# Moving the ten "low half" subtractions of the normalised rows from VectorE to GpSimd, and to another place in the written schedule

## Chip, cores and metric

One core of one Trainium2 chip runs the whole layer in one launch. The metric is the device time of the kernel in microseconds; lower is better.

## What is computed

x has 1250 rows (nodes) of 512. There are 20000 edges, `src` to `dst`, sorted by `dst`. Cut to what matters:

```python
xn  = layernorm(x)
agg = segment_sum(xn[src], dst)              # sum over the edges
h   = (1 + eps) * xn + agg
h   = relu(batch_norm(h @ W1 + b1)); h = relu(batch_norm(h @ W2 + b2))
q, k, v = elu(xn @ Wq + bq) + 1, elu(xn @ Wk + bk) + 1, xn @ Wv + bv
z   = 1 / (q . sum(k))                       # per head, 8 heads of 64
mix = (q @ (k^T v) * z) @ Wp + bp             # linear attention
x   = x + (xn + h) + mix
x   = x + moe(layernorm(x))                   # 64 experts, top 2 by hash
```

## The kernel before

**The front part.** Nodes lie in 10 row tiles (`NT`) of 128 (the last has 98). `XN` holds the normalised rows, `XT` their transpose. The aggregation is not a gather: for groups of edge tiles the kernel builds one-hot matrices and multiplies them into a matrix of edge counts `AT16` (1250 by 1250, 16 bit), and then multiplies the rows of x with it. The steps around the change:

- `oh` g (L965, on VectorE): one-hot of the destination key of edge group g, 16-bit `tensor_scalar`, one instruction for each edge tile of the group. For every third group the one-hot of the source, L969, is on VectorE too; for the others it is on ScalarE (L1362, L1365). `atm` g (L596, TensorE): their product. `ata` g (L984, VectorE): adds it from PSUM into `AT16`.
- K's products (`kmm` L562), `kadd` (L943) and `phi` (L949) on VectorE make phi(k). `phi` i also is a step of GpSimd: the running sum over the tiles, `KSUM` (L1536). `gmm` (L570) is the product of x's rows with phi(k).
- `ks` (L580, L585): sums of k on TensorE, after the last GpSimd addition. `ksc` (L953, L954): their copy from PSUM by VectorE; it frees the bank that the first product of Q needs.
- `qmm` (L607): Q's products, 12 units of four; `qphi` (L992) on VectorE ends each.
- `z` c (L618) and `zr` c (L1010): the denominators of attention and their reciprocal on VectorE, for each of three column chunks `CH` of 418, 416 and 416 nodes. `zb`, `zm` (L1023), `qzh`, `qzl` (L1028): z is spread and multiplied into Q.
- `xh` i (L1348, ScalarE): the row tile rounded to the reduced type float32r, `XNH`. `xl` i (L1002, VectorE): `XNL = XN - XNH`, the low half, 128 by 512. It is written where `XN` lies, so it has to wait for the `gmm` of its tile.
- `conv` (L1402, ScalarE) rounds the counts of a tile. `agg` c, i (L636, L637): eight products of tile i for chunk c, with `XNH` and with `XNL`. `ht` (L1035) takes the sums from PSUM.

**What sets the order.** `front_schedule` gives every step a due time, sorts the list, and every engine walks through the list and executes those of its steps that stand in it, in order. A due time orders and starts nothing: what starts a step is its semaphores and the engine being free. Numbers in it: K's products start at 12.0 with 6.0 for a tile, so `done` is 77.7; Q's units take 2.7 each; `agg` is due from `first` = 112.7, every 1.5. `xl` i is due at `base + turn * i - 1.7`, 111.0 and on, between the reciprocals. The last `phi` step is due before `done`.

The second part (from about 216 us) is the two dense layers with batch norm, the routing, and the experts with their weights streamed by SyncE's queue.

Of the kernel before, what the change touches and what calls it, by code (L numbers as in the profile page):

```python
# [11 lines left out]
ALU = mybir.AluOpType  # L12
# [4 lines left out]
NT = 10  # L17
# [21 lines left out]
def rows(i):  # L39
    return min(128, N - 128 * i)  # L40
# [30 lines left out]
def front_schedule():  # L71


    due = []

    def at(t, *step):
        due.append((t, len(due), step))

    begin, pair, unit, turn = 12.0, 6.0, 2.7, 1.5
    spent = 0  # L80
    at(11.2, "prep", 0)
    at(50.0, "prep", 1)
    work = [m * (33 + w) + 2 * (16 + w) for _, m, w in GRP]
    for g, w in enumerate(work):
        t = 13.6 + 96 * spent / sum(work)
        spent += w
        at(t - 2.3, "oh", g)
        at(t, "atm", g)
        at(t + 0.8, "ata", g)
    for i in range(NT):  # L90
        at(8.3 + 1.7 * i, "st", i)
    for q, (a, b) in enumerate(BATCH):
        at(8.3 + 1.7 * (b - 1) + 0.5, "sq" if q < ROOTS else "nwt", q)
        at(8.3 + 1.7 * (b - 1) + (0.9 if q < ROOTS else 5.0), "rr", q)
    for i in range(NT):
        k = begin + pair * i
        xt = k - (3.0 if i else 1.5)
        at(xt - 1.2, "xn", i)
        at(xt, "xt", i)
        at(xt + 1, "xtc", i)  # L100
        for q in range(4):
            at(k + pair * q / 8, "kmm", i, q)
            at(k + pair * (1.45 + q / 8), "gmm", i, q)
        at(k + pair / 2 + 0.3, "kadd", i)
        at(k + pair / 2 + 1.2, "kexp", i)
        at(k + pair / 2 + 2.4, "phi", i)
        at(k + pair / 2 + 3.2, "xh", i)
    done = begin + pair * (NT + 0.95)
    at(done + 0.1, "ks")
    at(done + 0.2, "gts")  # L110
    at(done + 0.9, "ksc")
    for u in range(12):
        t, r, c = done + 2.2 + unit * u, u % 4, u // 4
        for q in range(4):
            at(t + unit * q / 4, "qmm", r, c, q)
        at(t + unit + 0.2, "qact", r, c)
        at(t + unit + 1.9, "qphi", r, c)
    first = max(done + 2.2 + 12 * unit, 111.5) + 0.4
    at(first - 4.0, "flag")
    at(first - 2.5, "flagd")  # L120
    for c in range(3):
        base = first + 10 * turn * c
        for i in range(NT):
            if c == 0:
                at(base + turn * i - 1.7, "xl", i)
            at(base + turn * i - 2.0, "conv", c, i)
            at(base + turn * i, "agg", c, i)
        zb = base + (3.5 if c else 2.5)
        at((first - 7, first - 3.5, first + 9)[c], "z", c)
        at((first - 6, first - 2.5, first + 10)[c], "zr", c)  # L130
        at(zb, "zb", c)
        for r in range(4):
            t = zb + 1 + 1.6 * r
            at(t, "zm", r, c)
            at(t + 0.7, "qzh", r, c)
            at(t + 1.6, "qzl", r, c)
            t = base + 10 * turn + 0.5 + 0.8 * r
            at(t, "ht", r, c)
            at(t + 0.5, "hth", r, c)
            at(t + 1.04, "htl", r, c)  # L140
    last = first + 30 * turn
    at(last - 11, "kvt")
    at(last - 7.4, "kvd")
    for r in range(4):
        at(last - 6 + 0.9 * r, "m", r)
        at(last - 5 + 0.9 * r, "mh", r)
        at(last - 4 + 0.9 * r, "ml", r)
    at(last + 0.3, "wide")
    at(last + 4.2, "widev")
    for i in range(NT):  # L150
        at(last + 0.4 + 2.6 * i, "p", i)
        at(last + 4.3 + 2.6 * i, "pa", i)
    for t in range(8):
        at(last + 4.4 + 2.6 * t, "w1h", t)
        at(last + 5.4 + 2.6 * t, "w1l", t)
    return [step for _, _, step in sorted(due)]
# [101 lines left out]
def gnn_mix_moe(nc, x_in, edg_in, chk_in, wcol_in, low_in, w1g, w2g, wqkvp, hp_in, vec_in, brow_in, cst_in, we_in, out):  # L258
# [4 lines left out]
    with ExitStack() as ctx:  # L263
# [7 lines left out]
        V, A, G = nc.vector, nc.scalar, nc.gpsimd  # L271
# [9 lines left out]
        def big(first, size):  # L281
            return BIG1[:, first:first + size] if first < SPLIT else BIG2[:, first - SPLIT:first - SPLIT + size]

        def rounded(first, size):
            q = max(k for k in range(len(ROUND)) if cuts[k] <= first)
            return ROUND[q][:, first - cuts[q]:first - cuts[q] + size]

        def by(ap, k):
            return ap.rearrange("p (k n) -> p k n", k=k)
# [49 lines left out]
        XN, XNL, XNH = by(big(XN0, 5120), NT), by(rounded(XN0, 5120), NT), by(rounded(XN0 + 5120, 5120), NT)  # L339
        XNHf, XNLf = XNH.bitcast(F32), XNL.bitcast(F32)  # L340
# [122 lines left out]
        plan = bank_plan(order)  # L463
# [5 lines left out]
        full = [sem(f"full{b}") for b in range(8)]  # L469
# [407 lines left out]
        def vector(dve):  # L877
            done = [0]
# [12 lines left out]
            for step in order:  # L891
                kind = step[0]
# [27 lines left out]
                elif kind == "st":  # L920
                    i, n = step[1], rows(step[1])
# [12 lines left out]
                elif kind == "kadd":  # L934
                    i = step[1]
# [9 lines left out]
                elif kind == "phi":  # L945
                    i, n = step[1], rows(step[1])
# [9 lines left out]
                elif kind == "oh":  # L956
# [4 lines left out]
                    if g >= OHG:  # L961
                        b, use = at_of(("at", g - OHG))
# [23 lines left out]
                elif kind == "qphi":  # L986
                    r, c = step[1:]
                    o, w = CH[c]
                    b, use = at_of(("q", r, c))
# [1 line left out]
                    dve.wait_ge(moved[b], use)  # L991
                    V.scalar_tensor_tensor(QT[:, r, o:o + w], TMP[:, 2 * (r % 2) + 1, 0:w], 1.0, QT[:, r, o:o + w], ALU.min,  # L992
                                           ALU.max).then_inc(s_q, 1)
                elif kind == "xl":
                    i, n = step[1], rows(step[1])
                    dve.wait_ge(s_xh, i + 1)
                    if i < NT - 1:
                        dve.wait_ge(s_g, i + 1)
                    else:
                        b, use = plan["gts"][3]  # L1000
                        dve.wait_ge(full[b], use)
                    V.tensor_tensor(XNL[0:n, i, :], XN[0:n, i, :], XNHf[0:n, i, :], ALU.subtract).then_inc(s_xl, 1)  # L1002
                elif kind == "zr":
                    c = step[1]
                    b, use = at_of(("z", c))
# [5 lines left out]
                elif kind == "flagd":  # L1011
                    b, use = at_of(("flag",))
# [30 lines left out]
                elif kind == "kvd":  # L1043
                    b, use = at_of(("kvt",))
# [86 lines left out]
            for t in range(4):  # L1131
# [7 lines left out]
                if t == 1:  # L1139
                    b, use = at_of("hpm")  # L1140
# [45 lines left out]
            for step in route_order():  # L1186
                kind = step[0]
                if kind == "am":
                    a, e = ARGMAX[step[1]]
                    m = slice(4 * a, 4 * e)  # L1190
                    b, use = at_of(("lg", e - 1))
# [10 lines left out]
            b, use = at_of("near")  # L1202
# [8 lines left out]
            b, use = at_of("slots0")  # L1211
# [5 lines left out]
            for q, (i, e) in enumerate(((0, 8), (8, NT))):  # L1217
                b, use = at_of(f"below{q}")
# [84 lines left out]
            for i in range(NT + 1):  # L1303
                if i < NT:
                    n = rows(i)
# [212 lines left out]
        def gpsimd(pool):  # L1518
# [7 lines left out]
            for step in order:  # L1526
                kind = step[0]
                if kind == "phi":
                    i, n = step[1], rows(step[1])
                    u = PHI[i % 4][0:n, :]  # L1530
                    pool.wait_ge(s_phi, i + 1)
                    if i == 0:
                        G.tensor_copy(KSUM[:, :], u).then_inc(s_ksum, 1)
                    else:
                        pool.wait_ge(s_ksum, i)
                        G.tensor_tensor(KSUM[0:n, :], KSUM[0:n, :], u, ALU.add).then_inc(s_ksum, 1)  # L1536
                elif kind == "nwt":
                    q, w = slice(*BATCH[step[1]]), BATCH[step[1]][1] - BATCH[step[1]][0]
                    v, t, half, y = NWV[:, 0, 0:w], NWV[:, 1, 0:w], NWV[:, 2, 0:w], RR[:, q]
                    done = NEWTON * (step[1] - ROOTS)  # L1540

                    def newton(ins):
                        nonlocal done
                        done += 1
                        ins.then_inc(s_nwt, 1)
                        pool.wait_ge(s_nwt, done)

                    pool.wait_ge(s_st, BATCH[step[1]][1])
                    newton(G.tensor_scalar(v, MV[:, q, 1], 0.5, 0.5e-5, ALU.mult, ALU.add))
                    newton(G.tensor_scalar(y.bitcast(I32), v.bitcast(I32), -0.5, float(0x5f3759df - 2 ** 22), ALU.mult, ALU.add))  # L1550
                    for _ in range(3):
                        newton(G.tensor_tensor(t, y, y, ALU.mult))
                        newton(G.tensor_tensor(t, t, v, ALU.mult))
                        newton(G.tensor_tensor(t, half, t, ALU.subtract))
                        newton(G.tensor_tensor(y, y, t, ALU.mult))
                elif kind == "wide":
                    pool.wait_ge(s_key, NKEY["flag"])
                    far = pool.value_load(FLAGI[0:1, 0:1], min_val=0, max_val=2000)
                    with pool.If(far >= WIN):
                        wide_pool(pool)  # L1560

            b, use = at_of(("m", 3))
# [4 lines left out]
            b, use = at_of(("h1", 7, 2))  # L1567
# [24 lines left out]
            b, use = at_of("slots0")  # L1592
# [6 lines left out]
            b, use = at_of("slots")  # L1599
            pool.wait_ge(moved[b], use)  # L1600
            pool.wait_ge(sd_yz, 16 * 20)
            for r in range(32 - LATE):
                scatter_pair(r)
                n = r + LEAD
# [399 lines left out]
```

## Time and profile before

| what | value |
|---|---|
| device time, median of 3 runs | 557.75 us (556.35 to 559.13) |
| profiled execution | 558.88 us, span 557.1 us |
| granted clock of TensorE, mean | 0.994 of full speed |
| busy: TensorE, VectorE, ScalarE, GpSimd | 524.2, 348.0, 253.1, 92.7 us |
| moved by DMA | 105.69 MB, mean 190 GB/s |

Busy times are sums over the whole span. An engine that is busy 94% of it sets the time; the others matter through what it waits for. Since the stages have different limits, the table tells little of one stage: that is read from the rows below.

### The profile page before, as it was taken

The numbers are of one execution on the slowest core, as the hardware profiler recorded it, in microseconds if no ns is written. First come the engines' busy times: TensorE is split into PE (matmuls) and PEld (weight loads), VectorE is DVE, ScalarE is ACT, GpSimd is POOL, SyncE is SP. The second block draws the span as 40 slices with busy tenths as digits, with TensorE's granted clock in tenths as the row PEclk, the third lists the DMA queues.
The fourth block names the chain that finished last, engine by engine and source line by source line (L and its number), as shares of the span: only waits on it lengthen the run. The fifth ranks groups of instructions, "written<-read, shape, count | busy, mean of one in ns | idle before, by whom it ended". The sixth has DMA issues, their size and how long they took to land.

```text
span 557.1 us, 8514 instructions
## 1 busy us (share of the span) xinstructions
PE 524.2 (94%) x2810; PEld 362.6 (65%) x2810; DVE 348.0 (62%) x981; ACT 253.1 (45%) x554; POOL 92.7 (17%) x119
## 2 busy tenths in 40 slices
PE   0799999999998999999999999997999999999997
PEld 0344444455488888899999999985555554545545
DVE  4888787767876545638888234388344445344767
ACT  2787766676544533125665222347333334333300
POOL 4141101100000000000000000003144444445310
PEclk9999999999999999999999999999799999999999
DMA  8500000000020006465007322987999999999978
GB/s 301 209 2 1 1 1 1 1 1 0 2 77 0 1 0 214 166 237 207 2 0 281 136 75 77 349 348 278 338 406 416 414 415 412 413 416 415 400 267 310
DMA packets 32409, 105.69 MB, mean 190 GB/s; under 512 B 4640, under 2 KB 10017, under 8 KB 25324
## 3 DMA queue, kind: packets, MB, share of 16 engines
q1 hardware_dynamic: 22364, 86.09, 39.8%
q0 software_dynamic: 4880, 9.78, 4.7%
q10 hardware_dynamic: 5120, 9.25, 4.7%
q8 instruction: 24, 0.39, 0.3%
q14 instruction: 21, 0.17, 0.1%
HBM read 93.48 MB, written 17.84 MB: 200 GB/s over the span
## 4 chain that ended last, share of the span: by engine, by line
PE 77%; DMA 8%; DVE 7%; issue 5%; POOL 1%; DVEq 1%; ACT 1%; SPq 0%; POOLq 0%; ACTq 0%
PE PS L533 8%; PE PS L532 8%; PE PS L534 8%; PE PS L834 7%; PE PS L848 6%; PE PS L607 6%; DMA BIG<-xx_rows,TIDX 6%; PE PS L570 5%; PE PS L562 5%; PE PS L636 4%; PE PS L637 4%; PE PS L753 3%; PE PS L596 3%; PE PS L824 2%; DMA KSUM<-xx_rows,TIDX 2%
## 5 line engine op out<-in xcount | busy, mean ns | idle before, releaser
L532 PE MATMUL PS<-ROUND 128*128 128x416 f32 (+3 forms) x232 | 83.8, 361 | 0.0
L533 PE MATMUL PS<-ROUND 128*128 128x416 f32 (+3 forms) x232 | 83.5, 360 | 0.0
L534 PE MATMUL PS<-ROUND 128*128 128x416 f32 (+3 forms) x232 | 83.4, 359 | 0.0
L848 PE MATMUL PS<-BIG 128*64 128x512 f32 x208 | 52.8, 592 | 0.2 <-DVE BIG L1271 0.2
L1085 DVE BATCH_NORM_STATS2 BST<-BIG 128x6 f32<-128x416 f32 (+1 forms) x36 | 20.7, 590 | 44.0 <-ACT BIG L1448 35.5
L636 PE MATMUL PS<-ROUND 128*128 128x416 f32 (+3 forms) x120 | 43.5, 363 | 2.3 <-DVE ROUND L1002 1.8
L984 DVE TENSOR_TENSOR BIG<-PS,BIG 128x280 f32 (+17 forms) x69 | 30.7, 445 | 23.4 <-PE PS L596 19.4
L532 PEld LDWEIGHTS PS<-ROUND 128*128 128x128 f32 (+1 forms) x232 | 43.6, 188 | 2.6
L534 PEld LDWEIGHTS PS<-ROUND 128*128 128x128 f32 (+1 forms) x232 | 43.6, 188 | 2.5
L533 PEld LDWEIGHTS PS<-ROUND 128*128 128x128 f32 (+1 forms) x232 | 43.5, 188 | 2.4
L965 DVE TENSOR_SCALAR BIG<-BIG 128x180 f16<-128x180 f16 (+20 forms) x157 | 43.1, 321 | 0.0
L637 PE MATMUL PS<-ROUND 128*128 128x416 f32 (+3 forms) x120 | 42.2, 351 | 0.0
L562 PE MATMUL PS<-BIG 128*128 128x512 f32 (+1 forms) x80 | 41.3, 628 | 0.7 <-ACT BIG L1344 0.7
L570 PE MATMUL PS<-BIG 128*128 128x512 f32 (+1 forms) x80 | 39.9, 596 | 0.0
L596 PEld LDWEIGHTS PS<-BIG 128*128 128x128 f16 x157 | 14.1, 98 | 37.7 <-issue 23.6
L607 PE MATMUL PS<-BIG 128*128 128x416 f32 (+1 forms) x96 | 37.4, 515 | 0.2 <-DVE KSUM L953 0.2
L1289 DVE TENSOR_TENSOR BIG<-PS,BIG 128x512 f32<-128x512 f32 x21 | 14.5, 689 | 33.7 <-PE PS L848 33.7
L1480 ACT ACTIVATE BIG<-BIG 128x512 f32<-128x512 f32 x24 | 15.1, 629 | 43.7 <-DMA BIG<-xx_rows,TIDX 43.6
L1362 ACT ACTIVATE BIG<-BIG 128x128 f16<-128x128 f16 x103 | 34.6, 389 | 0.4 <-PE PS L596 0.4
L596 PE MATMUL PS<-BIG 128*128 128x180 f16 (+20 forms) x157 | 28.3, 274 | 4.8 <-DVE BIG L984 3.4
L834 PE MATMUL PS<-BIG,KSB 128*64 128x256 f32 x208 | 29.0, 405 | 0.7 <-issue 0.7
L1579 POOL DMA_INDIRECT y_rows<-BIG,SCIDX x21 | 22.0, 1050 | 43.4 <-DVE BIG L1289 43.4
(271 smaller groups left out, 967.5 us busy)
## 6 DMA issues: line engine op xcount, KB each, us to landing
BIG<-in_we SPq DMA_DIRECT2D x46, 1024.0 KB
BIG<-in_we SPq DMA_DIRECT2D x12, 512.0 KB
y_rows<-KVB SPq DMA_DIRECT2D x19, 256.0 KB
BIG<-y_rows SPq DMA_DIRECT2D x9, 512.0 KB, 9.2
EXTRA<-in_we SPq DMA_DIRECT2D x4, 1024.0 KB
XA<-in_we SPq DMA_DIRECT2D x4, 1024.0 KB
BIG<-in_wqkvp ACTq DMA_DIRECT2D x3, 1024.0 KB, 15.0
XA<-in_we SPq DMA_DIRECT2D x6, 512.0 KB
```

Source lines behind the costliest of these rows:

```text
L532: mm(o, ah, bh, start=first, stop=False)
L533: mm(o, ah, bl, start=False, stop=False)
L534: return mm(o, al, bh, start=False, stop=last)
L562: ins = mm(PS[0:n, b, :], XT[:, k, cs], WK[:, k, :], start=(k == 0), stop=(k == 3))
L570: ins = mm(PS[:, 4 + k, :], XN[0:n, i, 128 * k:128 * k + 128], PHI[i % 4][0:n, :], start=(i == 0), stop=(i == NT - 1))
L596: ins = mm(PS[:, b, 0:NT * w], SRCOH[:, g % OHG, q, :], KEYOH[:, g % OHG, NT * w * q:NT * w * (q + 1)], start=(q == 0), stop=(q == m - 1))
L607: ins = mm(PS[:, b, 0:w], WQ[:, k, f], XT[:, k, o:o + w], start=(k == 0), stop=(k == 3))
L636: mm(PS[:, b, 0:w], XNH[0:n, i, f], ATR[j % 3][0:n, 0:w], start=(i == 0), stop=False)
L637: ins = mm(PS[:, b, 0:w], XNL[0:n, i, f], ATR[j % 3][0:n, 0:w], start=False, stop=(i == NT - 1))
L834: ins = mm(PS[64 * j:64 * j + 64, b, 0:256], XTT[s][:, 128 * k + 64 * j:128 * k + 64 * j + 64], weights(2 * r + j, 256 * k, 256), start=(k ...
L848: ins = mm(PS[64 * j:64 * j + 64, b, :], HT[:, s, 128 * f2 + 64 * j:128 * f2 + 64 * j + 64], weights(2 * r + j, 1024 + 512 * f2, 512), sta ...
L965: V.tensor_scalar(KEYOH[:, g % OHG, NT * w * q:NT * w * (q + 1)], IOTA16[:, 0:NT * w], KEYF[:, t0 + q:t0 + q + 1], None, ALU.is_equal).the ...
```

## The change

In the schedule the ten `xl` get other due times: `done + 2.4 + 2.7 * i`, that is 80.1 and on, one for each of the first ten units of Q's products. And the step moves, with its waits unchanged, from VectorE's program to GpSimd's.

```diff
             if c == 0:
-                at(base + turn * i - 1.7, "xl", i)
+                at(done + 2.4 + 2.7 * i, "xl", i)
...
-                elif kind == "xl":
-                    i, n = step[1], rows(step[1])
-                    dve.wait_ge(s_xh, i + 1)
-                    if i < NT - 1:
-                        dve.wait_ge(s_g, i + 1)
-                    else:
-                        b, use = plan["gts"][3]
-                        dve.wait_ge(full[b], use)
-                    V.tensor_tensor(XNL[0:n, i, :], XN[0:n, i, :], XNHf[0:n, i, :], ALU.subtract).then_inc(s_xl, 1)
...
+                elif kind == "xl":
+                    i, n = step[1], rows(step[1])
+                    pool.wait_ge(s_xh, i + 1)
+                    if i < NT - 1:
+                        pool.wait_ge(s_g, i + 1)
+                    else:
+                        b, use = plan["gts"][3]
+                        pool.wait_ge(full[b], use)
+                    G.tensor_tensor(XNL[0:n, i, :], XN[0:n, i, :], XNHf[0:n, i, :], ALU.subtract).then_inc(s_xl, 1)
```

## Rows read from the trace of the kernel before

**Rows 1.** The page: busy time by engine, and the chain that ended last.
```profile
PE 524.2 (94%) x2810; PEld 362.6 (65%) x2810; DVE 348.0 (62%) x981; ACT 253.1 (45%) x554; POOL 92.7 (17%) x119
...
PE 77%; DMA 8%; DVE 7%; issue 5%; POOL 1%; DVEq 1%; ACT 1%; SPq 0%; POOLq 0%; ACTq 0%
```

**Rows 2.** Busy time by stretch: stretch, its us, then each engine, clock, DMA.
```profile
110.00:152.00 42.00, 41.22 (x147) 20.45 (x145) 31.83 (x82) 24.51 (x57) 0.00 (x0) 1.00 0.00 1
152.00:171.00 19.00, 16.85 (x92) 14.49 (x93) 13.84 (x21) 8.46 (x16) 0.00 (x0) 1.00 0.18 56
171.00:216.00 45.00, 44.34 (x239) 39.57 (x238) 26.96 (x49) 21.48 (x43) 1.03 (x3) 1.00 0.04 11
```

**Rows 3.** Whom TensorE waited for, 100 to 260 us: total, times, longest.
```profile
PE PS L636 <- DVE ROUND L1002: 1.8, 1, 1.8
PE PS L596 <- DVE BIG L984: 1.8, 2, 1.1
```

**Rows 4.** The instructions of line 1002: shortest, median, longest in ns; first and last start.
```profile
L1002 DVE TENSOR_TENSOR ROUND<-BIG,ROUND x10: 627/686/686, 151.6 to 168.5; 128x512 fp32r<-128x512 f32 x9, 98x512 fp32r<-98x512 f32 x1
```

**Rows 5.** Timeline of TensorE: start, us, line and operation, [idle before, released by].
```profile
103.64 0.48 PE L596 MATMUL PS<-BIG 128*128 128x360 f16 x2 [1.11 <-DVE BIG L984]
...
109.53 1.64 PE L607 MATMUL PS<-BIG 128*128 128x418 f32 x4 [0.23 <-DVE KSUM L953]
...
148.83 3.06 PE L607 MATMUL PS<-BIG 128*128 128x416 f32 x8
152.37 0.43 PE L636 MATMUL PS<-ROUND 128*128 128x418 f32 x1 [0.48 <-issue]
...
168.76 0.43 PE L636 MATMUL PS<-ROUND 128*128 128x418 f32 x1 [1.78 <-DVE ROUND L1002]
```

**Rows 6.** Timeline of VectorE around the reciprocals.
```profile
148.96 2.76 DVE L1010 RECIPROCAL KVB<-PS 128x416 f32<-128x416 f32 x1 [0.63 <-PE PS L618]
151.64 0.63 DVE L1002 TENSOR_TENSOR ROUND<-BIG,ROUND 128x512 fp32r<-128x512 f32 x1
...
165.31 2.76 DVE L1010 RECIPROCAL XG<-PS 128x416 f32<-128x416 f32 x1 [1.81 <-PE PS L618]
167.99 1.22 DVE L1002 TENSOR_TENSOR ROUND<-BIG,ROUND 128x512 fp32r<-128x512 f32 x2
```

**Rows 7.** Timeline of GpSimd.
```profile
25.29 0.61 POOL L1553 TENSOR_TENSOR BIG<-BIG 128x3 f32<-128x3 f32 x1
...
26.92 0.19 POOL L1553 TENSOR_TENSOR BIG<-BIG 128x3 f32<-128x3 f32 x1
...
84.00 1.27 POOL L1536 TENSOR_TENSOR KSUM<-KSUM,BIG 128x512 f32<-128x512 f32 x1 [6.24 <-DVE BIG L949]
91.86 1.27 POOL L1536 TENSOR_TENSOR KSUM<-KSUM,BIG 128x512 f32<-128x512 f32 x1 [6.59 <-DVE BIG L949]
101.43 1.52 POOL L1536 TENSOR_TENSOR KSUM<-KSUM,BIG 98x512 f32<-98x512 f32 x1 [8.30 <-DVE BIG L949]
```

**Rows 8.** Timeline of VectorE beside GpSimd's instructions and away from them.
```profile
25.17 0.68 DVE L949 SCALAR_TENSOR_TENSOR BIG<-BIG 128x512 f32<-128x512 f32 x1
...
83.84 1.53 DVE L965 TENSOR_SCALAR BIG<-BIG 128x300 f16<-128x300 f16 x2
...
86.00 0.50 DVE L965 TENSOR_SCALAR BIG<-BIG 128x320 f16<-128x320 f16 x2
...
92.25 0.49 DVE L984 TENSOR_TENSOR BIG<-PS,BIG 128x320 f32 x1 [0.47 <-PE PS L596]
```

**Rows 9.** Timeline of VectorE from 101 us to the copy of k's sum.
```profile
101.27 0.53 DVE L965 TENSOR_SCALAR BIG<-BIG 128x360 f16<-128x360 f16 x2
101.72 1.45 DVE L969 TENSOR_SCALAR BIG<-BIG 128x128 f16<-128x128 f16 x2
...
105.28 0.53 DVE L965 TENSOR_SCALAR BIG<-BIG 128x380 f16<-128x380 f16 x2
...
108.69 0.69 DVE L953 COPY KSUM<-PS 128x512 f32<-128x512 f32 x1 [1.79 <-PE PS L585]
```

## The prediction, made before the change was run

> **What bounds the kernel now.** I read the page first. TensorE is busy 94% of the span, and 77% of the chain that ended last lies on it [rows 1]. So an edit on VectorE or GpSimd moves the end only by making TensorE wait more or less. Next, the stages. In the stretch of Q's products (110 to 152 us) TensorE is busy 41.22 of 42.00 us, and VectorE 31.83, with GpSimd quite idle. In the first aggregation chunk (152 to 171) TensorE is busy 16.85 of 19.00 [rows 2]. Third, the list of who waited for whom between 100 and 260 us: TensorE waited 1.8 us for L984 (VectorE's adds of edge counts, `ata`), with 1.11 us of it just before 103.64, and 1.8 us, once, for L1002, which is `xl`, the operation that moves [rows 3, 5]. Last, the timelines around these waits. The reader is to see two things: VectorE is late in two places of the aggregation because of its long reciprocals, and it is also late just before Q's products, when GpSimd works beside it.
>
> **What the change removes.** Ten subtractions of 0.63 to 0.69 us leave VectorE [rows 4], some 6.9 us of its time. What they cost TensorE is read at two places [rows 5, 6].
>
> The first `agg` product starts at 152.37 after 0.48 us of idle time. On VectorE the reciprocal `zr` 1 runs from 148.96 for 2.76 us, to 151.72, and `xl` 0 comes behind it, from 151.64 to 152.27; TensorE starts 0.10 us later. Q's last products run from 148.83 for 3.06 us, to 151.89, and the reciprocal, which frees a bank that `agg` needs, is done before that. So without `xl` 0 behind the reciprocal, the 0.48 us go.
>
> The second place: `agg` 7 ends at about 168.76 - 1.78 = 166.98, `zr` 2 runs from 165.31 for 2.76 us, and `xl` 8 follows at 167.99; `agg` 8 starts at 168.76 after a wait of 1.78 us. `xl` 9 is then 0.6 us behind and not waited for. Without `xl` this wait goes whole: the converted counts for `agg` 8 come from ScalarE, which is 8.46 us busy in these 19 us [rows 2], and no other VectorE result is asked for there. The gain is 0.48 + 1.78 = 2.26 us. The other eight `xl` cost TensorE nothing, so taking them off VectorE gives nothing more. TensorE is nearly without idle time behind it (44.3 of 45 us in the stretch after 171), so I let the 2.26 us reach the end in full.
>
> **What the change adds.** GpSimd executes its steps in the order of the written schedule. The last step before `xl` on its queue is `phi` 9, the sum of k, which ends at 101.43 + 1.52 = 102.95 [rows 7]. What `xl` 0 to 8 wait for (the rounded copy by ScalarE and the G products on rows 0 to 8) is there by then, and `xl` 9's last G product is over by 107. The due times 2.7 us apart order the queue but start nothing. So the ten do not spread over Q's products: they run one behind the other from 102.95. The nearest row for one is L1536, the same shape with two inputs from SBUF and one output to it: 1.27 us each [rows 7]. Ten are 12.7 us, up to 115.65 or a little later, 36 us before the first `agg` asks. As a result nobody waits for them. No DMA is issued by `xl`, and behind it on GpSimd's queue only `wide` follows, which stays idle for 90 us more.
>
> What they cost is VectorE's time beside them. The pair of one-hots L965 that ran beside the GpSimd addition at 84.00 took 1.53 us, against 0.50 for the pair at 86.00 [rows 7, 8]: the second one stood still until GpSimd's addition ended. The nine additions of the trace all repeat this; beside seven of them, this one among them, the pair is 0.87 to 1.09 us longer. The plain add L984 at 92.25 took its ordinary 0.49 us beside the addition at 91.86: it reads one input from PSUM and is not touched. And the other way round, GpSimd's 3-element multiplication at 25.29 took 0.61 us, against 0.19 at 26.92, while L949 (two inputs from SBUF) ran from 25.17 to 25.85.
>
> The Trainium skill, page "SBUF — State Buffer", section "Who interferes with whom", says that VectorE in a two-port mode, or with two SBUF inputs, and a reading GpSimd instruction exclude each other for a whole instruction, whoever is first. By that page the "free" engine is not free beside `oh`, and the trace agrees (1.53 against 0.50 us).
>
> Where does that land? VectorE's queue at 101.72 still holds, in this order [rows 9]: the pair L969 (1.45 us beside `phi` 9), `ata`, a pair L965, `ata`, a pair, `ata`, two pairs (the L965 at 105.28 and an L969 pair behind it), `ata`, and then L953, the copy of k's sum, at 108.69, for which Q's first product waited 0.23 us [rows 5]. So nine instructions that exclude GpSimd's (one left of L969's pair, and four pairs) stand ahead of the instruction that opens Q's products. VectorE had 1.79 us of idle time just before L953; that is its whole slack.
>
> How GpSimd and VectorE take turns when GpSimd has work without a gap, no row shows. Bounds from both sides:
> - Strict turns: each GpSimd end (104.22, 105.49, ... every 1.27 us) lets one of the nine pass. The ninth passes at 102.95 + 9 x 1.27 = 114.38, the last `ata` takes 0.5, and the copy comes at about 115.0 instead of 108.69: 6.3 us.
> - Pairs pass together, as at 101.27, where two L965 went through and the addition that began at 101.43 came out 0.25 us late [rows 7, 9]. Then five GpSimd instructions at most are waited for. The steps are: L969 at 104.2, `ata`, pair after 105.5, `ata` to 106.4, pair after 106.9, `ata` to 107.9, four L965/L969 after 108.4, `ata`, copy at about 110.0. That is 1.3 us, and the five `xl` left over cost about 0.5 more in the next 6 us, where VectorE has idle stretches of 1.1 and 0.6 us. Sum 1.8 us.
>
> The second of a pair starts 0.22 us behind the first, and its race with the next GpSimd instruction is close: at 84.00 GpSimd won it, at 101.43 VectorE did, with the same spacing. I take half of the pairs split: (6.3 + 1.8) / 2 = 4.05 us. TensorE has no slack in Q's products, so all of it reaches TensorE.
>
> **Sum.** -2.26 + 4.05 = +1.8 us. The profiled execution (558.88 us, span 557.1) goes to about 560.7; it is 1.1 above the median of the runs. On the median 557.75 I forecast 559.5 us. The runs before spread over 2.8 us, 0.5%, and that is about what can be told from no change.
>
> **Rivals.**
> *Nothing reaches TensorE.* The exclusion costs VectorE time but its slack takes it. Against it: TensorE already waits 1.11 us for L984 before 103.64 [rows 5], and what held L984 up is the pair L969 beside a single GpSimd addition. Time: 557.75 - 2.26 = 555.5 us. It decides if the copy L953 starts before about 109.
> *VectorE is locked out until GpSimd's row of ten ends.* One addition leaves a gap today; ten without a wait between them may leave none. VectorE then resumes at 115.65 and has the 3.8 us of work from 103.1 to 106.9 ahead of it, so the copy is at 119.5: 10.8 us late. Time: 557.75 - 2.26 + 10.8 = 566.3 us. Against it: the pair that stood waiting at 101.72 was through, both of it, at 103.17, 0.22 us after GpSimd's end [rows 9], so what waits gets in at the first opening.
> *GpSimd's subtraction is slower than its addition.* Its output is the rounded type, which no GpSimd instruction of this trace has. With 1.6 us in place of 1.27 and strict turns, nine turns add 9 x 0.33 = 3.0 to the 6.3: 557.75 - 2.26 + 9.3 = 564.8 us. It decides by the duration of one `xl` on GpSimd.
>
> **How the numbers follow.** The forecast case, turns that are partly strict, has 0.70, and its own range is the two bounds, 557.3 (-2.26 + 1.8) to 561.8 (-2.26 + 6.3). Nothing reaches TensorE: 0.13. Locked out: 0.08. Slower subtraction: 0.09. The range 555.0 to 564.0 takes in the first rival with the scatter of the runs, and leaves out the lock-out and the worst of the slow subtraction. Slower by over 0.5% (above 560.5): a third of the forecast case (0.23) and most of the last two, 0.38. Faster by over 0.5% (below 555.0) would need more than the whole gain: 0.06. Within: 0.56.
>
> **What the profile after would show.** Ten GpSimd instructions in a row from about 103 to 116 to 118, 1.27 to 1.5 us each. L965 and L969 between 103 and 116 drawn out to over 1 us, L984 not. The copy L953 at 110 to 115, and Q's first product just behind it. No wait of TensorE at the first `agg` and at `agg` 8. The forecast is wrong if the ten are spread out, if VectorE stands still for ten microseconds in one piece, or if the two waits in the aggregation stay under another name.

## The result, and the profile after

The changed kernel takes 563.33 us (median of 6 runs, 561.02 to 565.30), the kernel before 557.54 (6 runs). The ratio is 1.0096, with a 95% interval of 1.0063 to 1.0130: slower by 5.4 us (3.5 to 7.3), where 1.8 were forecast. The two medians alone lie 5.8 us apart. The profiled execution took 562.01 us with a span of 560.2, and its mean granted clock is 0.988, against 0.994 before.

GpSimd's timeline around the moved work, columns as in [rows 7]; L1527 is `phi`, L1536 is now `xl`:

```profile
101.09 1.52 POOL L1527 TENSOR_TENSOR KSUM<-KSUM,BIG 98x512 f32<-98x512 f32 x1 [8.30 <-DVE BIG L949]
102.57 12.34 POOL L1536 TENSOR_TENSOR ROUND<-BIG,ROUND 128x512 fp32r<-128x512 f32 x10
```

The ten run in one row behind `phi` 9 and not over Q's products, and the row has no gap: ten in 12.34 us is 1.22 to 1.23 us from start to start. The instructions themselves:

```profile
L1536 POOL TENSOR_TENSOR ROUND<-BIG,ROUND x10: 1256/1268/1277, 102.6 to 113.6; 128x512 fp32r<-128x512 f32 x9, 98x512 fp32r<-98x512 f32 x1
```

One takes 1.27 us, the duration of the additions of [rows 7]. The rounded output costs nothing, and VectorE delayed none of them: the longest is 0.02 us over the shortest. VectorE beside them, which answers to [rows 9]:

```profile
101.37 2.50 DVE L969 TENSOR_SCALAR BIG<-BIG 128x128 f16<-128x128 f16 x2
103.80 0.50 DVE L984 TENSOR_TENSOR BIG<-PS,BIG 128x340 f32 x1
104.22 2.17 DVE L965 TENSOR_SCALAR BIG<-BIG 128x360 f16<-128x360 f16 x2
106.31 0.52 DVE L984 TENSOR_TENSOR BIG<-PS,BIG 128x360 f32 x1
106.76 2.10 DVE L965 TENSOR_SCALAR BIG<-BIG 128x360 f16<-128x360 f16 x2
108.78 0.52 DVE L984 TENSOR_TENSOR BIG<-PS,BIG 128x360 f32 x1
109.22 2.12 DVE L965 TENSOR_SCALAR BIG<-BIG 128x380 f16<-128x380 f16 x2
111.27 2.47 DVE L969 TENSOR_SCALAR BIG<-BIG 128x128 f16<-128x128 f16 x2
113.66 0.52 DVE L984 TENSOR_TENSOR BIG<-PS,BIG 128x360 f32 x1
114.10 0.67 DVE L953 COPY KSUM<-PS 128x512 f32<-128x512 f32 x1
```

Every pair of one-hots takes 2.1 to 2.5 us, in place of 0.53 or less (1.45 for the first, which already ran beside `phi` 9), and each of its two instructions took 0.87 to 1.32 us, so each waited for a GpSimd instruction of its own. The plain adds L984 took their 0.5 us untouched. The copy L953 comes at 114.10. This execution was 0.34 us ahead of the one before at `phi` 9 (101.09 against 101.43), so the copy is 5.75 us late.

TensorE, which answers to [rows 5]:

```profile
104.36 0.48 PE L596 MATMUL PS<-BIG 128*128 128x360 f16 x2 [2.17 <-DVE BIG L984]
104.67 2.29 PE L570 MATMUL PS<-BIG 98*128 98x512 f32 x4
...
114.24 0.82 PE L596 MATMUL PS<-BIG 128*128 128x380 f16 x2 [2.80 <-DVE BIG L984]
114.92 3.13 PE L607 MATMUL PS<-BIG 128*128 128x418 f32 x4
...
155.73 0.91 PE L618 MATMUL PS<-BIG,EXTRA 128*32 128x416 f32 x8
156.56 3.06 PE L607 MATMUL PS<-BIG 128*128 128x416 f32 x8
159.14 0.67 PE L636 MATMUL PS<-ROUND 128*128 128x418 f32 x1
...
181.51 0.98 PE L653 MATMUL PS<-KVB,BIG 32*128 32x416 f32 x8
```

Three things are to be seen. The waits of the aggregation (0.48 and 1.78 us in [rows 5]) are gone. Ahead of Q's products TensorE now waits 2.17 and 2.80 us for the edge counts, against 1.11 in [rows 5]. And Q's first four products took 3.13 us, against 1.64 for the same four in [rows 5], with no wait in them. The busy times by stretch (columns as in [rows 2]: the figure behind GpSimd's count is the granted clock) say why:

```profile
100.00:106.00 6.00, 3.83 (x14) 1.48 (x12) 6.00 (x9) 2.90 (x8) 4.91 (x4) 1.00 0.00 1
106.00:110.00 4.00, 4.00 (x8) 1.61 (x7) 4.00 (x6) 1.48 (x4) 4.00 (x5) 0.57 0.02 4
110.00:112.00 2.00, 1.44 (x11) 0.91 (x9) 2.00 (x3) 1.94 (x7) 2.00 (x2) 1.00 0.00 0
112.00:120.00 8.00, 5.76 (x11) 2.78 (x12) 5.99 (x16) 0.26 (x1) 2.91 (x3) 0.57 0.00 0
120.00:124.00 4.00, 4.00 (x15) 2.10 (x14) 1.80 (x7) 3.18 (x8) 0.00 (x0) 1.00 0.00 0
```

TensorE's clock fell to the lower of its two levels (1.2 in place of 2.4 GHz) in parts of 106 to 110 and of 112 to 120, each time after TensorE had stood for one of the long waits or during it. The kernel before has the full clock in this whole part:

```profile
98.00:160.00 62.00, 59.51 (x228) 32.16 (x227) 47.13 (x118) 37.77 (x86) 1.52 (x1) 1.00 0.06 18
```

Three landmarks of TensorE give the balance. Before, the second `z` product (L618) starts at 147.99 and the second `zb` (L653) at 176.51:

```profile
147.99 0.91 PE L618 MATMUL PS<-BIG,EXTRA 128*32 128x416 f32 x8
...
176.51 0.98 PE L653 MATMUL PS<-KVB,BIG 32*128 32x416 f32 x8
```

| stretch | before | after | difference |
|---|---|---|---|
| `phi` 9 on GpSimd to Q's first product | 8.10 | 13.83 | +5.73 |
| Q's first product to the second `z` | 38.46 | 40.81 | +2.35 |
| second `z` to second `zb` (it holds both waits) | 28.52 | 25.78 | -2.74 |
| sum | | | +5.34 |

The three stretches are read from one execution of each kernel. Their sum agrees with the measured difference, 0.0096 x 557.5 = 5.35 us, closer than the interval (3.5 to 7.3) can tell. The two profiled spans differ by 3.1 us only. The clock also fell in the expert stage of both, for longer in the execution before (mean 0.91 in the first row, before, against 0.96 in the second, after), which goes the right way to explain that; how much of it this makes was not worked out:

```profile
380.00:420.00 40.00, 34.77 (x290) 19.34 (x288) 19.82 (x67) 17.99 (x51) 14.45 (x14) 0.91 0.91 340
```

```profile
380.00:420.00 40.00, 35.00 (x307) 21.81 (x307) 23.68 (x82) 21.36 (x56) 13.61 (x14) 0.96 0.89 329
```

That drop is there without the change, and the mean clock of the kernel before differs from run to run: 0.987 to 1.000 in one series of 31 runs, which took 554.5 to 562.3 us. I count it as scatter.

### The profile page after: what moved, and what is told of

The parts are those of the page before. It is cut to its first block, busy times and chain, and to the rows that moved or that the text cites. A ratio compares the mean times of both kernels' runs of the same rounds, so it can differ in the third digit from the quotient of the medians.

```text
span 560.2 us, 8513 instructions
## 1 busy us (share of the span) xinstructions
PE 526.4 (94%) x2809; PEld 363.8 (65%) x2810; DVE 349.6 (62%) x971; ACT 252.5 (45%) x554; POOL 105.0 (19%) x129
## 4 chain that ended last, share of the span: by engine, by line
PE 77%; DVE 9%; DMA 7%; issue 4%; DVEq 1%; POOL 1%; ACT 1%; SPq 0%; POOLq 0%; ACTq 0%
PE PS L533 8%; PE PS L532 8%; PE PS L534 8%; PE PS L834 7%; PE PS L848 7%; PE PS L607 6%; PE PS L570 5%; PE PS L562 4%; PE PS L636 4%; PE PS L637 4%; DMA BIG<-xx_rows,TIDX 4%; PE PS L753 3%; PE PS L596 3%; PE PS L824 2%; DMA KSUM<-xx_rows,TIDX 2%
## 5 line engine op out<-in xcount | busy, mean ns | idle before, releaser
L965 DVE TENSOR_SCALAR BIG<-BIG 128x180 f16<-128x180 f16 (+20 forms) x157 | 47.9, 352 | 0.0
L984 DVE TENSOR_TENSOR BIG<-PS,BIG 128x280 f32 (+17 forms) x69 | 30.6, 444 | 25.0 <-PE PS L596 21.2
L596 PEld LDWEIGHTS PS<-BIG 128*128 128x128 f16 x157 | 14.1, 99 | 42.2 <-issue 24.2
L607 PE MATMUL PS<-BIG 128*128 128x416 f32 (+1 forms) x96 | 39.5, 539 | 0.0
L596 PE MATMUL PS<-BIG 128*128 128x180 f16 (+20 forms) x157 | 29.5, 281 | 8.1 <-DVE BIG L984 6.2
L834 PE MATMUL PS<-BIG,KVB 128*64 128x256 f32 x224 | 29.2, 385 | 0.0
```

What stands on the lines that cost most here:

```text
L596: ins = mm(PS[:, b, 0:NT * w], SRCOH[:, g % OHG, q, :], KEYOH[:, g % OHG, NT * w * q:NT * w * (q + 1)], start=(q == 0), stop=(q == m - 1))
L607: ins = mm(PS[:, b, 0:w], WQ[:, k, f], XT[:, k, o:o + w], start=(k == 0), stop=(k == 3))
L834: ins = mm(PS[64 * j:64 * j + 64, b, 0:256], XTT[s][:, 128 * k + 64 * j:128 * k + 64 * j + 64], weights(2 * r + j, 256 * k, 256), start=(k ...
L965: V.tensor_scalar(KEYOH[:, g % OHG, NT * w * q:NT * w * (q + 1)], IOTA16[:, 0:NT * w], KEYF[:, t0 + q:t0 + q + 1], None, ALU.is_equal).the ...
```

## The experiments

Theory: -2.7 us are the gain of taking `xl` off VectorE; GpSimd's row without a gap lets one excluding VectorE instruction pass for each of its own, which costs 5.7 us ahead of the copy of k's sum, and TensorE's clock, lowered by its standing still, 2.3 more. Rivals: the real subtractions' data or what follows them is to blame; ten exclusions cost the same wherever they lie; the clock fell for a reason of its own.

### The gain alone: `e_none`

```diff
-                    V.tensor_tensor(XNL[0:n, i, :], XN[0:n, i, :], XNHf[0:n, i, :], ALU.subtract).then_inc(s_xl, 1)
+                    V.tensor_copy(DUM[:, i:i + 1], ONE).then_inc(s_xl, 1)
...
-                        ins = mm(PS[:, b, 0:w], XNL[0:n, i, f], ATR[j % 3][0:n, 0:w], start=False, stop=(i == NT - 1))
+                        ins = mm(PS[:, b, 0:w], XNH[0:n, i, f], ATR[j % 3][0:n, 0:w], start=False, stop=(i == NT - 1))
```

> The kernel before without the low halves: each of the ten subtractions is replaced by a copy of one column, and the aggregation multiplies with the high half twice, so TensorE has the same products and the low halves are left out. It gives the whole of what taking the subtractions off VectorE can win. Theory (the gain is the two waits and the restarts behind them): -2.7 us, TensorE's waits at the first aggregation product and at tile 8 gone. Rival (the waits are only put off to the next late operation): under -1 us.

555.53 us (median of 10), ratio 0.9962 (0.9936 to 0.9988): -2.1 us. Of the two waits of the aggregation only the first was gone, so the run doesn't show the whole gain, as it was meant to. TensorE's timeline:

```profile
167.58 0.43 PE L637 MATMUL PS<-ROUND 128*128 128x418 f32 x1 [1.26 <-DVE DUM L1003]
```

The one-column copy stands where `xl` 8 stood, behind the reciprocal, and TensorE waited 1.26 us for it. Of 1.78 us only 0.52 went; the reciprocal's part of the wait stayed. So most of this wait was not the subtraction's 0.69 us, but its place in VectorE's queue. From the second `z` to the second `zb` this execution takes 27.48 us, against 28.52 before and 25.78 in the changed kernel: 1.04 us less, 0.52 at each of the two places. The measured -2.1 us (interval -3.6 to -0.7) can't tell 1.0 from 2.7.

### The cost alone: `e_extra`

```diff
...
+                elif kind == "extra":
+                    i = step[1]
+                    to = ([EXTRA[:, 512 * q:512 * q + 512] for q in range(4)] + [big(RW0 + 512 * q, 512) for q in range(4)]
+                          + [XG4[:, :], big(AT0 + 6400, 512)])[i]
+                    G.tensor_tensor(to, CST[:, 0:512], CST[:, 128:640], ALU.subtract).then_inc(s_dum, 1)
```

> The kernel before, with its ten subtractions left on VectorE, and ten more subtractions of the same shape (inputs from a constant table, outputs to unused space) on GpSimd behind the last sum of k, where the change has its own. It gives the cost alone. Theory (strict turns with VectorE's one-hots, then a lowered clock): the copy of k's sum 5.7 us later, +8 us in all, of which 2.3 us are from the clock. Rival (the added time comes from the data or the rounded type of the real subtractions, or from something behind them): under +4 us.

565.36 us (median of 4), ratio 1.0136 (1.0096 to 1.0177): +7.6 us. The edit also has two waits, not shown, that keep VectorE and ScalarE off the space the ten write until they are done. The copy of k's sum is at 114.59, with `phi` 9 at 101.57, so it is 5.76 us late. This is made by ten idle subtractions of a constant table, so it has nothing to do with x's rows, the rounded type or what waits for `xl`. TensorE in this run (L598 and L986 are L596 and L984 of the other kernels):

```profile
104.84 0.48 PE L598 MATMUL PS<-BIG 128*128 128x360 f16 x2 [2.17 <-DVE BIG L986]
107.38 0.48 PE L598 MATMUL PS<-BIG 128*128 128x360 f16 x2 [0.34 <-DVE BIG L986]
114.73 0.81 PE L598 MATMUL PS<-BIG 128*128 128x380 f16 x2 [4.03 <-DVE BIG L986]
```

Here the clock fell only behind the second long wait (mean 0.72 from 112 to 124 us, and 1.00 to 110), and that wait is longer, 4.03 us, because TensorE came to it faster. I read from it that the first drop of the changed kernel cost nothing and only shortened the next wait; this is argued from the two profiles, no run has that drop alone. One more loss of this profiled execution comes 60 us behind the row: after the wait of 1.78 us in the aggregation, which this kernel still has, the clock fell again (mean 0.83 from 176 to 186 us), and the stretch from the second `z` to the second `zb` is 1.56 us longer than before. In the execution before, the same wait was not followed by a drop [rows 2].

### The schedule's half alone, on VectorE: `e_dve_q`

```diff
-                at(base + turn * i - 1.7, "xl", i)
+                at(done + 2.4 + 2.7 * i, "xl", i)
```

> Only the new due times, the subtractions stay on VectorE: one for each unit of Q's products. Theory (VectorE has 10 us of slack in Q's products, but little at any one place): most of the 2.7 us gain stays, -1 to -2.5 us; no GpSimd in it, so the copy of k's sum stays at about 108.5 and the clock at full. Rival (VectorE is as short of time as it was beside GpSimd, 6.9 us more of work delay the one-hots): 0 to +3 us.

555.28 us (median of 8), ratio 0.9958 (0.9928 to 0.9987): -2.3 us. TensorE waited for VectorE before 150 us as in the kernel before (1.11, 0.23 and 0.67 us) and at no `agg`. From the second `z` to the second `zb` it takes 25.78 us, as in the changed kernel, so this run has the whole gain of 2.74. On VectorE the new due times do spread the ten, from 110.50 to 140.39, since its queue has steps between them; on GpSimd's queue they are next to one another whatever their due times.

### The ten on GpSimd, really spread: `e_spread`

```diff
                     pool.wait_ge(s_xh, i + 1)
+                    pool.wait_ge(s_q, i + 1)
```

> The changed kernel with one more wait: subtraction i on GpSimd waits until Q's unit i is done, so that the ten really spread over Q's products. Theory (it is the row of ten without a gap, at the place where VectorE has no slack, that costs): each holds up one VectorE instruction by about 1 us, which the slack takes, the copy of k's sum at 108.5, clock at full, -2 to -2.7 us. Rival (ten exclusions of 1 us cost TensorE wherever they lie): +2 to +6 us.

555.80 us (median of 12), ratio 0.9953 (0.9928 to 0.9979): -2.6 us. VectorE's timeline beside the subtractions at 120.20 and 122.47:

```profile
120.76 1.07 DVE L965 TENSOR_SCALAR BIG<-BIG 128x420 f16<-128x420 f16 x2
...
122.74 1.36 DVE L965 TENSOR_SCALAR BIG<-BIG 128x420 f16<-128x420 f16 x2
124.47 0.60 DVE L984 TENSOR_TENSOR BIG<-PS,BIG 128x420 f32 x1 [0.37 <-PE PS L596]
```

The exclusion is the same (1.07 and 1.36 us for a pair), but between two subtractions VectorE catches up (it is idle again for 0.37 us behind the second pair), and TensorE waited no more than in the kernel before. The rival that ten exclusions cost the same wherever they lie falls.

### TensorE kept busy while it waits: `e_fill`

```diff
...
+                if step == ("atm", 45):
+                    b, use = at_of(("ks",))
+                    pe.wait_ge(moved[b], use - 1)
+                    fill_bank(b, FILL_A)
+                elif step == ("atm", 48):
+                    b, use = plan["gts"][3]
+                    pe.wait_ge(moved[b], use)
+                    fill_bank(b, FILL_B)
```

> The changed kernel with products that nobody reads, put into TensorE's queue at the two places where it waits for VectorE (2 products of 512 columns before the counts' product 45, 5 before product 48), so that it doesn't stand still. VectorE and GpSimd do the same as in the changed kernel. Theory (2.3 us of the loss come from TensorE's clock, which fell after it had stood still): granted clock 1.00 from 100 to 160 us, Q's first product at about 114.5 to 115.5, 2 to 2.7 us faster than the changed kernel, so +2.5 to +3.5 us against the kernel before. Rival (the clock falls for another reason): the same drops, +5 us or more.

559.76 us (median of 10), ratio 1.0051 (1.0029 to 1.0073): +2.8 us, that is 2.5 less than the changed kernel, with the same work on VectorE and GpSimd. TensorE's timeline (L545 is the filler, L620 Q's products) and the clock:

```profile
110.23 4.45 PE L545 MATMUL PS<-BIG 128*128 128x512 f32 x10
114.52 0.49 PE L609 MATMUL PS<-BIG 128*128 128x380 f16 x2
115.13 1.64 PE L620 MATMUL PS<-BIG 128*128 128x418 f32 x4
```

```profile
112.00:120.00 8.00, 7.88 (x25) 3.79 (x24) 6.70 (x17) 1.39 (x4) 3.12 (x3) 1.00 0.00 0
```

Q's first four products start as late as in the changed kernel and take 1.64 us at a granted clock of 1.00. From there to the second `z` it is 38.45 us, against 40.81 in the changed kernel and 38.46 before. So the clock's 2.35 us came from TensorE having stood still.

### The row of ten behind the copy: `e_after_copy`

```diff
                     pool.wait_ge(s_xh, i + 1)
+                    pool.wait_ge(moved[plan[("ks",)][1][0]], plan[("ks",)][1][1])
```

> The changed kernel with one more wait: the row of ten starts only when VectorE has copied k's sum, at about 109.5, so no one-hot ahead of that copy is held up, but the ten still run without a gap. Theory A (only the place ahead of the copy is costly, since VectorE has idle stretches behind it): under +1 us. Theory B (a gapless row gives VectorE one excluding instruction in 1.27 us, too few wherever it lies: some 20 of them are due in these 12.7 us against 2.8 us of idle time): TensorE waits 3 to 5 us for the one-hots between 111 and 125, perhaps with a lowered clock, +1 to +4 us.

560.66 us (median of 10), ratio 1.0051 (1.0019 to 1.0083): +2.8 us, as theory B had it. TensorE:

```profile
111.91 0.50 PE L596 MATMUL PS<-BIG 128*128 128x380 f16 x2 [0.43 <-DVE BIG L984]
...
115.18 0.34 PE L596 MATMUL PS<-BIG 128*128 128x380 f16 x1 [0.50 <-DVE BIG L965]
...
120.11 0.50 PE L596 MATMUL PS<-BIG 128*128 128x400 f16 x2 [3.19 <-DVE BIG L969]
```

It waited 0.43 + 0.50 + 3.19 = 4.1 us for one-hots. Behind the last of these waits the clock fell once more (mean 0.72 from 120 to 126 us). Together the stretch from Q's first product to the second `z` is 6.3 us longer than before (44.78 against 38.46). So VectorE's idle time behind the copy takes little of a gapless row: ahead of the copy the row cost 5.73 + 2.35 = 8.1 us, behind it 6.3. It is the row more than its place that costs.

### A small gap between the ten: `e_chain`

```diff
                     pool.wait_ge(s_xh, i + 1)
+                    if i:
+                        pool.wait_ge(s_xl, i)
```

> The changed kernel, but each subtraction on GpSimd waits for the one before it, which leaves about 0.1 us between them. It asks whether the pairs of one-hots, 0.22 us apart, get through together when GpSimd's row has gaps. Theory (the next GpSimd instruction is already queued when VectorE's first gets in, a gap of 0.1 us changes nothing): pairs of 2.1 us as in the changed kernel, copy of k's sum at about 114 to 115, +5 to +6 us. Rival (a small gap lets the second one in): pairs of about 1.3 us, copy at 110 to 112, 0 to +3 us.

556.75 us (median of 10), ratio 0.9972 (0.9945 to 1.0000): -1.6 us, where my theory had +5 to +6. The rival was right about the pairs and the copy; its time, 0 to +3 us, was a little too high (the interval is -3.1 to 0.0). GpSimd and VectorE in the same place:

```profile
102.50 1.26 POOL L1538 TENSOR_TENSOR ROUND<-BIG,ROUND 128x512 fp32r<-128x512 f32 x1
104.25 12.80 POOL L1538 TENSOR_TENSOR ROUND<-BIG,ROUND 128x512 fp32r<-128x512 f32 x9 [0.50 <-POOL ROUND L1538]
```

```profile
104.15 1.53 DVE L965 TENSOR_SCALAR BIG<-BIG 128x360 f16<-128x360 f16 x2
105.60 0.52 DVE L984 TENSOR_TENSOR BIG<-PS,BIG 128x360 f32 x1
106.04 1.26 DVE L965 TENSOR_SCALAR BIG<-BIG 128x360 f16<-128x360 f16 x2
...
107.67 1.11 DVE L965 TENSOR_SCALAR BIG<-BIG 128x380 f16<-128x380 f16 x2
108.70 1.42 DVE L969 TENSOR_SCALAR BIG<-BIG 128x128 f16<-128x128 f16 x2
...
110.47 0.68 DVE L953 COPY KSUM<-PS 128x512 f32<-128x512 f32 x1
```

GpSimd now takes 1.42 us from start to start (12.80 / 9) in place of 1.22. With these 0.2 us more the second one-hot of a pair gets in as well: pairs of 1.1 to 1.5 us, not 2.1 (all but the first, which stands beside `phi` 9 and the first subtraction and takes 2.51), and the copy comes at 110.47, 2.2 us late after the 0.41 us by which this execution is ahead. No wait of TensorE exceeds 2.17 us, and its clock stays full here (1.00 from 98 to 160 us). By the landmarks this execution is even with the one before up to the second `zb` (+2.18, +0.54 and -2.74 us in the three stretches), so the trace doesn't show where the measured 1.6 us come from. The very work of the changed kernel, at the same place and later by 2 us at its end, is 6.9 us faster for one wait that changes no result.

### Only the place in VectorE's queue: `e_dve_early`

```diff
-                at(base + turn * i - 1.7, "xl", i)
+                at(base + turn * i - (5.0 if i else 3.55), "xl", i)
```

> The kernel before with only the due times of its subtractions changed, on VectorE: the first two go ahead of the second reciprocal and the last two ahead of the third, the others as before about. Theory (the gain belongs to two places where a subtraction stood behind a reciprocal): -2 to -2.7 us, as with all ten moved. Rival (the reciprocal comes later instead and its users wait): -1 to +1 us.

554.62 us (median of 10), ratio 0.9956 (0.9932 to 0.9981): -2.5 us. The subtractions ahead of the reciprocals cost little: the second reciprocal starts at 149.23, 0.5 us later than before (this execution is 0.23 ahead), and the stretch from the second `z` to the second `zb` is 26.05 us, 0.27 more than in `e_dve_q`. `e_dve_q`, `e_spread` and this one beat both kernels, and their intervals overlap: which is best isn't told apart.

## Why the prediction was right or wrong

The direction and the mechanism held; the size was off by 3.6 us (1.8 forecast, 5.35 measured), out of three terms. The median of 563.33 us lies within the range of 555.0 to 564.0, but only by 0.7 us, and that is partly luck: a term of 2.35 us was in none of the cases the range was made from. The likeliest outcome of the forecast, no change beyond 0.5% (0.56), did not come; the one it gave 0.38 did.

**What bounds the kernel, and what is removed: right, a little small.** Both waits went in full. They were worth 2.74 us and not 2.26. From the second `z` to the third (164.34 before, 171.35 after) the gain is 0.73 for the wait of 0.48, and from there to the second `zb` it is 2.01 for the wait of 1.78: about 0.24 us at each place that stands in no idle time. What these are made of no run shows. `e_dve_q`, `e_spread` and `e_dve_early`, which have neither wait, gained 2.3 to 2.6 us. `e_none` gained 2.1, but by its trace only 1.04 come from the two places. A single loose end: I wrote that the other eight `xl` cost TensorE nothing; `e_dve_early`, which keeps all of them on VectorE and gains 2.5 us, bears it out within its interval.

**The due times that order and start nothing: right.** The ten ran from 102.57 to 114.91; I had 102.95 to 115.65.

**The duration on GpSimd: right.** 1.27 us. The rival of a slower subtraction is out.

**Where the cost lands: right.** Nine one-hots ahead of the copy of k's sum, L984 untouched, the copy at 110 to 115: it came at 114.10. `e_extra`, with the real subtractions left on VectorE, has the same delay (5.76 us).

**"I take half of the pairs split": this step failed.** All were. The term is 5.73 us in place of 4.05, close to the bound of strict turns (6.3, less nine times the 0.05 us by which GpSimd's instructions overlap). The reason for my middle value was the close race at 84.00 and 101.43. But those were GpSimd instructions that came to an idle engine, and in a row the next one is queued already. `e_chain` shows what decides: a wait between GpSimd's instructions, 0.2 us more from start to start, gives the rest of the pair its turn. Its copy is 2.2 us late; my lower bound had 1.3.

**A term that I did not have: TensorE's clock, 2.35 us.** The working priced the waits of TensorE and not what the clock does after them. `e_fill` shows it: the waits filled with products all but 0.5 us at the first place, full clock, 2.5 us back. Without it the time would lie at about 561.0, inside the forecast case's own range (up to 561.8).

**The rivals.** That nothing reaches TensorE is refuted for this kernel (the copy came at 114.10, not before 109), but holds with the ten spread out (`e_spread`). The lock-out to the end of the row was wrong: one instruction passed in each turn. Its 566.3 us lie 3.0 above the measured median, the forecast of 559.5 lies 3.8 below: that it came nearer says nothing for it.

## What to carry to other kernels

Before work goes to an idle engine, ask which of the busy one's instructions exclude it, and what is due beside the place where it will really start; a due time in a written order starts nothing, and an engine with few steps runs them in one row. If the row must lie beside an engine that is late, break it: a wait between its instructions, or one that ties each to a step of the other engine, was worth 6.9 and 8.0 us here (ratios 0.9972 and 0.9953 against 1.0096). And where a wait stands behind a long instruction, try first to put the short one ahead of it in the same queue: here that gave as much as moving it, within what the runs can tell (`e_dve_early`, -2.5 us; `e_spread`, -2.6).

## What the runs showed of the hardware that I had not expected

- The row of ten GpSimd instructions without waits was not held up by VectorE's one-hots (12.34 us, each 1.26 to 1.28), while each of these took 0.87 to 1.32 us and only one passed between two of GpSimd's. With a semaphore wait between GpSimd's instructions the share turns: 1.42 us from start to start, and two of VectorE's get through. Whether the gap or the wait itself does it was not separated. The Trainium skill, page "SBUF — State Buffer", section "Who interferes with whom", has the exclusion, for the whole of an instruction; how the two take turns in a row is from these runs.
- TensorE's clock fell to 1.2 GHz after it had stood for 2.17 us before 104.36 and again around its wait of 2.80 us, in the changed kernel. In `e_extra` and `e_chain` the wait of 2.17 us at the same place was not followed by a drop. The wait of 1.78 us in the aggregation was followed by one in `e_extra` (mean clock 0.83 from 176 to 186 us) and by none in the kernel before. So one such wait doesn't always bring a drop; what decides was not tried.
